# A two-layer decoder on one core: GpSimd takes its statistics finishes earlier, between the expert gathers

## What is computed

```python
x = x + attn0(layernorm(x))             # 16 heads of width 8, 4 key heads
x = x + cross0(layernorm(x), ctx, ctx)
x = x + ffn0(layernorm(x))              # one shared expert, 8 routed, top 2
x = x + attn1(layernorm(x))             # 4 shared heads of width 64 with a position bias
x = x + cross1(layernorm(x), ctx, ctx, mask)
x = x + ffn1(layernorm(x))              # another mixture, 8 experts, top 2
```

```python
shared = silu(xt @ sg_w.T) * (xt @ su_w.T) @ sd_w.T
probs = sigmoid(xt @ router_w.T + routing_bias)
topk_p, topk_idx = top_k(probs, 2);  topk_p = topk_p / sum(topk_p)
y = (silu(xt @ wg[e].T) * (xt @ wu[e].T)) @ wd[e].T      # for each chosen expert e
out = shared + sum(topk_p * y)
```

## Time and profile before

| | us |
|---|---|
| median of three runs | 1168.65 |
| the profiled execution's own time | 1171.92 |
| its span in the trace | 1170.1 |
| TensorE busy | 1018.9 (87%) |
| VectorE busy | 901.3 (77%) |
| ScalarE busy | 677.5 (58%) |
| GpSimd busy | 628.0 (54%) |
| mean granted TensorE clock | 0.947 of full |

### The profile page before, as it was taken

How to read it: one execution, slowest core, us unless ns; L and a number is a source line. 1 busy time by engine, 2 the same in 40 slices (tenths; PEclk the granted TensorE clock), 3 DMA queues, 4 the chain that set the end, 5 groups by cost and what they waited for, 6 DMA issues and landing times.

```text
span 1170.1 us, 33353 instructions
## 1 busy us (share of the span) xinstructions
PE 1018.9 (87%) x10238; PEld 706.7 (60%) x10238; DVE 901.3 (77%) x2462; ACT 677.5 (58%) x1737; POOL 628.0 (54%) x956
## 2 busy tenths in 40 slices
PE   3799999999989887999877867978999999877997
PEld 2466666666657776777655646754555555555775
DVE  5588899888895796888867867764777777748896
ACT  1377787777776433554435546752566665646775
POOL 8667778876773445433344453157556751423554
PEclk9999999999996698999989989996999999979999
DMA  5765578966672001333321101015554551044550
GB/s 145 171 141 125 123 153 171 186 140 137 150 186 77 21 35 64 108 100 91 90 57 34 30 22 54 1 30 121 121 109 104 118 115 30 2 166 176 180 179 28
DMA packets 81442, 119.66 MB, mean 102 GB/s; under 512 B 16704, under 2 KB 62688, under 8 KB 80272
## 3 DMA queue, kind: packets, MB, share of 16 engines
q1 hardware_dynamic: 66688, 85.24, 30.5%
q0 software_dynamic: 9472, 27.27, 7.8%
q10 hardware_dynamic: 5136, 5.31, 2.3%
HBM read 80.75 MB, written 36.18 MB: 100 GB/s over the span
## 4 chain that ended last, share of the span: by engine, by line
PE 44%; DVE 17%; issue 15%; DMA 14%; POOL 6%; ACT 2%; SPq 1%; DVEq 1%; POOLq 0%; ACTq 0%
DMA experts_gathered<-experts_y_dram,experts_index 6%; PE heads_ps_pv L987 4%; PE heads_ps_max L965 4%; PE cross_ps_max L965 4%; DVE heads_neg_max L769 3%; PE cross_ps_pv L987 3%; DMA experts_xs_dram<-QK,experts_index 3%; PE cross_ps_max L955 3%; PE cross_ps_exp L958 2%; DMA QK<-heads_qk_parts 2%; DVE experts_hidden L1739 2%; PE experts_ps_gu L2451 2%; PE heads_ps_out L1049 2%; POOL experts_xs_dram L2142 1%; PE heads_ps_pv L1036 1%
## 5 line engine op out<-in xcount | busy, mean ns | idle before, releaser
L769 DVE TENSOR_REDUCE heads_neg_max<-heads_ps_max 128x4 f32<-128x512 f32 x256 | 169.3, 681 | 34.6 <-PE heads_ps_max L965 32.7
L843 ACT ACTIVATE heads_E<-heads_ps_exp 128x512 f32<-128x512 f32 x256 | 150.2, 604 | 22.4 <-PE heads_ps_pv L987 17.7
L769 DVE TENSOR_REDUCE cross_neg_max<-cross_ps_max 128x4 f32<-128x512 f32 x128 | 86.9, 686 | 49.6 <-PE cross_ps_max L965 48.9
L2156 POOL DMA_INDIRECT experts_gathered<-experts_y_dram,experts_index x64 | 61.8, 966 | 99.5 <-issue 69.9
L965 PE MATMUL heads_ps_max<-QK 48*128 48x128 bf16 x1024 | 102.1, 224 | 10.4 <-DMA QK<-heads_qk_parts 6.6
L969 PE MATMUL heads_ps_exp<-QK 50*128 50x128 bf16 x1024 | 103.0, 222 | 0.0
L2379 ACT ACTIVATE experts_act_out<-experts_ps_gu 128x256 f32<-128x256 f32 x110 | 42.3, 385 | 100.1 <-PE experts_ps_gu L2453 99.4
L843 ACT ACTIVATE cross_E<-cross_ps_exp 128x512 f32<-128x512 f32 x128 | 76.6, 599 | 40.5 <-PE cross_ps_exp L969 22.1
L2142 POOL DMA_INDIRECT experts_xs_dram<-QK,experts_index x64 | 61.5, 962 | 68.3 <-DMA experts_xs_dram<-QK,experts_index 52.6
L965 PEld LDWEIGHTS heads_ps_max<-QK 48*128 48x128 bf16 x1024 | 58.4, 96 | 51.6 <-issue 19.2
L987 PE MATMUL heads_ps_pv<-heads_E,heads_V 128*32 128x128 f32 x2048 | 84.9, 285 | 0.0
(11 more groups left out here) (323 smaller groups left out, 3238.4 us busy)
## 6 DMA issues: line engine op xcount, KB each, us to landing
experts_share<-experts_cT_dram SPq DMA_DIRECT2D x7, 2304.0 KB, 8.5
heads_qk_parts<-heads_parts POOLq DMA_DIRECT2D x32, 384.0 KB, 4.7
QK<-heads_qk_parts SPq DMA_DIRECT2D x64, 192.0 KB
QK<-heads_qk_parts SPq DMA_DIRECT2D x64, 128.0 KB
cross_qk_parts<-cross_parts POOLq DMA_DIRECT2D x16, 384.0 KB, 4.3
QK<-cross_qk_parts SPq DMA_DIRECT2D x32, 192.0 KB
experts_xs_dram<-load_stats SPq DMA_DIRECT2D x26, 192.0 KB, 2.9
experts_xs<-experts_xs_dram SPq DMA_DIRECT2D x78, 64.0 KB
```

Source lines behind the costliest of these rows:

```text
L769: nc.vector.tensor_reduce(neg_max[:, half, heads.start:heads.stop], ps_max[:, u % 2, :].rearrange("q (h k) -> q h k", h=HU), AX.X, ALU.max ...
L843: nc.scalar.activation(E[:, half, heads.start:heads.stop, :], ps_exp[:, u % 2, :].rearrange("k (h q) -> k h q", h=HU), ACT.Exp, scale=scal ...
L2156: pool.indirect_dma_start(gathered[n % GATHERS][:], None, y_dram[h], bass.IndirectOffsetOnAxis(index[:, choice, b:b + 1], 0)).then_inc(loa ...
```

## The change

Three things move. `finish(0)` and `finish(2)` go from ahead of the 13th pair of their half to ahead of the tenth. Three of the lead's finishes (steps 3, 5 and 7) go from behind the last gather to ahead of the pairs of batches 26, 28 and 30 (`B` is 32). And the first front goes one unit later, from u = 96 to 97; the second front follows it to 103, and `ONE_TURN` to 97. Nothing is added or taken away.

```diff
-    LEAD_UNIT, LEAD_ALONE, LEAD_MIX = UNITS_ALL - 14, -3, -2
+    LEAD_UNIT, LEAD_ALONE, LEAD_MIX = UNITS_ALL - 13, -3, -2
+    LEAD_TURNS = {B - 6: 3, B - 4: 5, B - 2: 7}
     LEAD_FRONT, ONE_TURN = (LEAD_UNIT, LEAD_UNIT + 6), LEAD_UNIT
...
             for b in range(h * HALF_B, (h + 1) * HALF_B):
-                if b == h * HALF_B + 12:
+                if b == h * HALF_B + 9:
                     finish(2 * h)
+                if b in LEAD_TURNS:
+                    ahead.lead.pool(At(None, LEAD_TURNS[b]))
                 for n in range(2 * b - 2, 2 * b):
                     if n >= 0:
                         pool.wait_ge(loaded[n % GATHERS], 16 * (n // GATHERS + 1))
...
             if h == 0:
                 finish(1)
-        for k in ahead.steps()[1:]:
+        for k in range(max(LEAD_TURNS.values()) + 1, ahead.steps().stop):
             ahead.lead.pool(At(None, k))
         finish(3)
```

## The result

| | kernel before | changed kernel |
|---|---|---|
| median of the runs | 1183.35 us (12 runs, 1162.44 to 1199.43) | 1161.22 us (12 runs, 1156.07 to 1174.41) |
| ratio to before, 95% interval | | 0.9898 (0.9870 to 0.9926) |
| profiled execution: time, span | 1171.92 us, 1170.1 | 1165.0 us, 1163.2 |
| last routed unit's result done | 618.56 us | 617.57 us |
| power of finish(3) starts | 710.8 us | 701.8 us |

The ratio leaves out of each set of runs what lies more than 1.5% above the set's own fastest, so one low run shifts it: of 36 runs of the kernel before, whose fastest took 1159.69 us, 24 are left out, and of 12 others of the same kernel (e1_base, fastest 1169.09 us) none. On the 1168.65 us of the start it gives 1156.7 us, 12.0 us less (8.6 to 15.2).

A forecast was written before the change was run, and what follows sets the result against it. VectorE's waits for GpSimd's late finishes (7.2, 6.7 and 2.2 us) were taken as the bound in the stretch changed; 6.1 + 0 + 0 + 7.8 = 13.9 us off 1168.65 gave 1154.8 us, range 1145 to 1165.

The forecast's parts named there:

- The anchor: The kernel before's median of 1168.65 us, from which the whole kernel's forecast saving of 13.9 us was subtracted.
- The chances: For the whole kernel's time: within 2% of no change 0.92, faster by over 2% 0.06, slower by over 2% 0.02.
- First term: First half: finish(0) moved early removes VectorE's 7.17 us wait, then gathers set the pace; gain 6.1 us.
- the bound of 9.4: First half, upper bound: if gathers did not hold the units, the stage would end at 609.2 and gain 9.4 us.
- the pair of batch 9 about 3.3 us behind that gather's start: Sign in the first half: batch 9's pair starts about 3.3 us after the start of batch 8's second gather.
- The second term: Lead's finishes between the last pairs: the 6.65 us wait and 1.2 us of low clock go; 7.8 us, ends 6.65 and 8.5.
- The terms of 0: Moving the front one unit later and finish(2) ahead of batch 25's pair were each costed at nothing.
- The third wait: End of the mixing: VectorE's 2.2 us wait for finish(3), which needs the last mix, was to stay.
- A (gain given back): Rival: gathers hold the units, first stage gains 1.9, second only 6.65, or part is lost; 1160.1 us, chance 0.18.
- C (slower, low clock): Rival: small idle gaps keep TensorE at 0.50 through the units and attention with gathers; 1173.7 us, chance 0.05.
- B (more than forecast): Rival: gathers keep up with the units, first stage gains 9.4 us, second 8.5; 1150.8 us, chance 0.15.
- The set-aside rule: Two-SBUF-input VectorE and SBUF-reading GpSimd instructions exclude each other; some tenths of a us for finish(0), taken as nothing.

The follow-up runs named there:

- e1_base: The kernel before run once more with no edit; 1180.02 us, ratio 1.0060.
- e10_finish2_late: The changed kernel with finish(2) back ahead of the 13th pair of its half; 1166.81 us, ratio 0.9916.
- e3_first_half: The kernel before with only finish(0) ahead of the tenth pair and the first front one unit later; 1176.31 us, ratio 1.0014.
- e4_second_half: The changed kernel with finish(0) and the front put back, so only finish(2) and the lead's three finishes are moved; 1167.78 us, ratio 0.9973.
- e7_two_pairs: The changed kernel with four gathers (two pairs) in flight instead of two; 1187.02 us, ratio 1.0097.
- e2_changed: The changed kernel run once more with no edit; 1161.26 us, ratio 0.9880.
- e11_changed: The changed kernel run a third time with no edit; 1161.43 us, ratio 0.9861.

## Why the prediction was right or wrong

**The anchor failed.** "on it the forecast is 1168.65 - 13.9": the three runs lay low for this kernel. Its 102 runs of this study have a median of 1178.4 us, 9.8 us higher, so the changed kernel's 1161.22 is 6.4 us above the forecast, though the saving was larger than forecast by the stages (15.6) and by all runs (17.1). Two errors of opposite sign, and a range made wide for the scatter, put it inside the range; that is luck.

**The chances failed, and this is the step that was wrong.** "A measurement of this kernel can tell about 2% from no change" was too coarse, and no row stood behind it. The interval of the ratio is 0.3% to either side and excludes 1. That interval alone says too little, since a kernel against itself excluded 1 as well, but the gain came out three times, at ratios of 0.9898, 0.9880 and 0.9861 and at 22.1, 18.4 and 16.7 us between the medians of all runs. So a gain of 1 to 1.5% is a measured gain, where the text had it as no difference with 0.92. Its own 13.9 us is 1.2% of 1168.65, and the ratio's 12.0 (8.6 to 15.2) holds it. The wrong step is the bound, not the sum.

**First term, 6.1 us: right.** B gives 5.9. The wait of 7.2 us is gone, and what it doesn't bring in full goes to the gathers, as argued. The projection put the end of the stage 612.5 - 605.35 = 7.15 us behind the start of batch 15's pair. In all nine profiles with `finish(0)` early and two gathers in flight it came 7.0 to 7.2 us behind it, in the slow first half of e10_finish2_late too (7.1); with the old order it was 12.4 to 13.0. But there wasn't much behind that limit: with three in flight B gained 1.9 more, 7.9 in all, short of the bound of 9.4, and VectorE's waits for gathers grew by 1.2, 1.8 and 0.1 us in the three profiles, not by 2 to 4.

"The moments have been there for 2.0 us by then" holds for the one profile it was read from, where some early gathers had landed late (batch 1's at 4.4 us). In e1_base, the same kernel, they come 0.2 us after the end of batch 8's second gather; in the three profiles of the changed kernel 0.03 us before, 0.4 and 0.1 us after it. `finish(0)` has gone to the earliest place that doesn't cost, with next to no margin. "the pair of batch 9 about 3.3 us behind that gather's start" was missed by 0.7 us (3.98).

**The second term, 7.8 us with ends 6.65 and 8.5, was mis-sized.** C gives 9.7. The mechanism held: step 11 follows at 5.28 us and the clock stays at 1.00. What failed is "this 1.2 us goes with the stall": both its numbers came from one execution. In the two other profiles with the old order there the wait was 8.53 and 8.43 us, since the gathers ended 1.6 and 1.7 us later against the end of B, and the low clock behind it took 3.3 and 3.2 us rather than 1.2. Against the profile that it was read from, the 7.8 fits (C 8.0).

**The terms of 0: right.** The front's unit (B 67.9 without the shift), finish(2) (C 84.7 without the move; mix(25) has no wait in front of it), and the lead's finishes between the pairs. The first of these had its power take 1.20 us, where 128 x 2 otherwise takes 0.71 in the median, and still fitted; the reason for the 1.20 stands below.

**The third wait stays: right**, 2.2 us.

**The rivals.** A (gain given back) falls with e3_first_half and e4_second_half: both parts keep what they bring. C (slower, low clock) falls with 1.00 in the windows of the changed kernel. Its dismissal leaned on a claim that is too wide, "the clock fell before only behind idle times of about 7 us": in the same profile TensorE was granted 0.50 from 370 to 390 us, where no wait of it from 330 to 420 us was longer than 3.2 us. B (more than forecast) is nearest in size, with 17.9 against 15.6 measured by stages, but by another way: the surplus is in the second stall, not in gathers that keep up.

**The set-aside rule.** The powers with which the prediction answered it don't test it: none of the VectorE instructions that ran beside them takes two inputs from SBUF, and none did beside the changed kernel's power of `finish(0)` (1.68 us). L1191 does, the product of `shared_E` and `shared_recip`. VectorE's timeline of the changed kernel, then GpSimd's:

```profile
660.46 0.73 DVE L1191 TENSOR_TENSOR shared_probs<-shared_E,shared_recip 128x512 f32<-128x512 f32 x1
...
665.76 0.69 DVE L1191 TENSOR_TENSOR shared_probs<-shared_E,shared_recip 128x512 f32<-128x512 f32 x1
```
```profile
660.61 0.64 POOL L298 TENSOR_TENSOR norm_mean<-experts_moments,norm_one 128x8 f32<-128x8 f32 x1
...
665.83 1.20 POOL L301 TENSOR_TENSOR norm_rstd<-norm_var_eps,norm_minus_half 128x2 f32<-128x2 f32 x1
```

The copy takes 0.64 us instead of 0.20 and ends 0.06 us behind L1191; the power takes 0.5 us more. Four more short operations of GpSimd that start inside an L1191, up to 760 us, take 0.64 to 0.66 us and end 0.05 us behind it. So the rule of the Trainium skill's page "SBUF — State Buffer", "Who interferes with whom", holds in this trace for L1191, and "The trace doesn't agree for this form" was a misreading. Beside the mixes' L2307, which reads two SBUF tiles as well, powers of 128 x 2 took their usual 0.69 to 0.71 us. The price here is tenths of a us within a landing gap, so the term of 0 stands.

## What to carry to other kernels

A small operation that others wait for belongs ahead of queued transfers, in the first landing gap behind the moment its input is ready; one slot earlier turned into a standstill of 4.5 us for everything behind it. Read the moment at which the input is ready from several profiles: here a margin of 2.0 us in one was 0.03 us or less in most others. A standstill's price is the standstill plus the time at the low clock behind it, and both vary between executions, so read them from more than one profile. Where the start of a program scatters by more than the change is worth, cut the profiles at marks around the change and compare the pieces, and take a few runs of the kernel before as a sample and not as its time.

## What the runs showed of the hardware

**The start scatters, and the clock in it.** A, in which the changed and the old kernel run the same instructions, ranged from 538.0 to 557.5 us (e7_two_pairs, whose gathers reach into it, apart). The windows of the kernel before, of e2_changed and of e11_changed:

```profile
360.00:420.00 60.00, 51.38 (x321) 42.40 (x319) 41.73 (x139) 26.57 (x56) 25.07 (x29) 0.69 0.07 24
```
```profile
360.00:420.00 60.00, 47.54 (x356) 39.03 (x349) 44.26 (x151) 27.78 (x60) 28.57 (x35) 0.82 0.10 33
```
```profile
360.00:420.00 60.00, 46.79 (x386) 38.26 (x384) 45.42 (x155) 29.79 (x63) 28.73 (x33) 0.87 0.15 49
```

In the same 60 us of the span TensorE was granted 0.69, 0.82 and 0.87, and got through 321, 356 and 386 matmuls. This stretch alone doesn't set A: the first of the three profiles has 543.7 us and the last 542.1, and the changed kernel's first, with 0.69 too, has 550.0. Which execution is granted what, and what else makes A vary, I can't say.

**Gathers of GpSimd back to back stop the others.** Eight in 8.81 us brought standstills of 3.3 us on ScalarE and of up to 4.1 us on SyncE at a DMA share of 0.32, the same as without them; three in flight brought none that the waits show. The cause is open.

**The landing decides, and it varies.** A pair behind `finish(0)` started 3.98, 4.34 and 4.28 us after the last gather ahead of it in the three profiles of the changed kernel, against 3.29 without the finish. The finish isn't what holds it: it was over 0.9 to 1.2 us before the pair started. The gather ahead of it landed 3.2, 3.6 and 3.5 us after its start, where the median is 2.6, and the pair came 0.7 to 0.8 us behind that landing, as pairs without a finish ahead of them do. Where the landing took 2.6 us, in e10_finish2_late, the pair came after 3.30 us with the same finish in the gap. Nor is it shown that the finish slows the landing: in e1_base the same gather took 3.6 us with no finish behind it. Why it is slow isn't known.
